# Router products with 32-column stationary matrices in the four quarters of the output partitions

## What is computed

```python
x = x + conv_ref(_ln_c(x), ...)       # sign of the centred x, 3x3 binary convolution, batch norm over all images, relu
t = _to_tokens(x)                     # 3136 tokens of 128 channels in each image
t = t + ffn_ref(_ln_t(t), ...)

def ffn_ref(x, ...):                  # x: 32 x 3136 x 128
    weights = (jnp.einsum('bsd,do->bso', x, wr) + br)[..., 0]    # the router: one number for each token
    _, idx = jax.lax.top_k(weights, k)                           # k = 1568
    sel_idx = idx[:, :kk]                                        # kk = 1567 tokens in each image
    h = jax.nn.gelu(jnp.einsum('bkd,dh->bkh', sel, w1) + b1)     # 128 -> 512
    y = jnp.einsum('bkh,hd->bkd', h, w2) + b2                    # 512 -> 128
    y = y * w_sel[..., None]                                     # times the router's number
    processed = jnp.zeros_like(x).at[batch_idx, sel_idx].set(y)
    return processed + x
```

## Time and profile before

| | |
|---|---|
| unprofiled executions | 2337.59, 2347.46, 2359.03 us |
| profiled execution, its own time | 2349.64 us |
| its span, first to last instruction | 2347.8 us |
| mean granted TensorE clock | 0.961 |
| TensorE busy | 2133.6 us (91%) |
| VectorE, ScalarE, GpSimd busy | 68%, 52%, 40% |

### The profile page before, as it was taken

One profiled execution on the slowest core, in us unless ns is written; L12 is line 12 of the kernel. 1 busy time (PEld: TensorE's weight loads), 2 busy tenths in 40 slices (PEclk: granted clock), 3 DMA queues, 4 the chain that ended last, 5 costly groups with the idle time before them and its releaser, 6 DMA issues. The chain is left out here.

```text
span 2347.8 us, 37567 instructions
## 1 busy us (share of the span) xinstructions
PE 2133.6 (91%) x9515; PEld 1079.1 (46%) x9515; DVE 1605.5 (68%) x4759; ACT 1219.9 (52%) x2030; POOL 944.6 (40%) x714
## 2 busy tenths in 40 slices
PE   6999999975999989899999989999999898989996
PEld 3555555542444444444444444444444444444442
DVE  6777777765667767667676766666666676767765
ACT  4444444434555555555555555565555555555553
POOL 1000000015455555555455545454555555545533
PEclk9999999997999999999999999999999999999998
DMA  4444444440232222223232223222223232223213
GB/s 148 165 164 159 155 156 156 154 164 26 95 117 101 101 101 101 107 107 106 105 115 101 101 101 126 96 108 101 102 101 115 107 116 101 101 101 112 101 61 114
DMA packets 68758, 268.17 MB, mean 114 GB/s; under 512 B 22352, under 2 KB 27184, under 8 KB 64688
## 3 DMA queue, kind: packets, MB, share of 16 engines
q1 hardware_dynamic: 59296, 215.50, 25.3%
q10 hardware_dynamic: 9360, 51.69, 6.0%
HBM read 188.08 MB, written 77.87 MB: 113 GB/s over the span
## 5 line engine op out<-in xcount | busy, mean ns | idle before, releaser
L943 PE MATMUL ps<-hs,w_c 128*128 128x448 f32 x1792 | 797.4, 571 | 0.6 <-ACT yo L505 0.6
L495 ACT ACTIVATE hs<-ps,b1c,undo 128x448 f32<-128x448 f32 x896 | 601.3, 719 | 166.6 <-PE ps L934 166.4
L412 POOL TENSOR_TENSOR tl<-tr,th 128x448 f16<-128x448 f32 x224 | 248.5, 1110 | 580.9 <-ACT th L525 472.3
L943 PEld LDWEIGHTS ps<-hs,w_c 128*128 128x128 f32 x1792 | 328.5, 198 | 218.0 <-issue 178.9
L860 PE MATMUL ps<-yo,cwT 128*128 128x448 bf16 x2016 | 425.7, 356 | 0.0
L505 ACT ACTIVATE yo<-ps,cols 128x448 f32<-128x448 f32 x224 | 141.8, 633 | 408.5 <-PE ps L943 408.3
L419 POOL TENSOR_TENSOR yo<-yo,base 128x448 f32<-128x448 f32 x224 | 285.9, 1282 | 134.0 <-DVE yo L787 134.0
L932 PE MATMUL ps<-th,w_h 128*128 128x448 f16 x896 | 326.0, 364 | 0.0
L934 PE MATMUL ps<-th,w_l 128*128 128x448 f16 x896 | 324.9, 363 | 0.0
L933 PE MATMUL ps<-tl,w_h 128*128 128x448 f16 x896 | 324.4, 362 | 0.0
L693 DVE TENSOR_TENSOR ur<-xb,ps 128x448 f32<-128x448 f32 x224 | 138.5, 619 | 263.9 <-PE ps L923 249.2
(11 more groups left out here) (125 smaller groups left out, 2578.0 us busy)
## 6 DMA issues: line engine op xcount, KB each, us to landing
xb<-x SPq DMA_DIRECT2D x31, 1568.0 KB, 7.5
xb<-x SPq DMA_DIRECT2D x33, 896.0 KB, 4.7
gate_all<-gate_row ACTq DMA_DIRECT2D x32, 896.0 KB, 4.4
result<-yo SPq DMA_DIRECT2D x32, 896.0 KB, 3.9
y_int<-y SPq DMA_DIRECT2D x32, 784.0 KB, 3.7
xb<-x SPq DMA_DIRECT2D x33, 672.0 KB, 4.4
gate_all<-gate_row ACTq DMA_DIRECT2D x32, 672.0 KB, 5.6
result<-yo SPq DMA_DIRECT2D x32, 672.0 KB, 3.0
```

The lines of the kernel that those rows point to most:

```text
L412: nc.gpsimd.tensor_tensor(cut(tl, c), tr[(b + c) % 2][:, :], cut(th, c), ALU.subtract).then_inc(tl_ready, 1)
L495: nc.scalar.activation(hs[(b + slot) % 2][:, j, :], ps[:, H_BANK + j, 0:T], ACT.Gelu_apprx_tanh, bias=b1c[:, j:j + 1], scale=undo[:, 1:2]) ...
L943: last = M(bank, w2_c[:, j, :], hs[(b + c) % 2][:, j, :], start=first, stop=final)
```

## The change

The stationary matrices of the router become 32 columns wide (COLS), cut from `wsel_h` and `wsel_l` of 64 columns. The seven chunks are taken in two parts: chunks 0 to 3 at position 17 and chunks 4 to 6 at position 25. Within a part, chunk q writes to the output partitions 32q to 32q + 31 of the same bank, and the four (or three) chunks are issued one behind the other for each of the three pairs of operands. Part 0 leaves its results on partitions 0, 32, 64, 96, part 1 on 1, 33, 65. `take_router` copies all 128 partitions, at position 26 instead of 28. The write of `wrow` to DRAM becomes two DMAs, of four and of three rows that lie 32 partitions apart, and the queue waits for both. The number of products stays 21.

```diff
+COLS = 32
+NQ = C // COLS
-ROUTER_AT = [15, 16, 17, 20, 21, 23, 27]
+ROUTER_AT = [17, 25]
-        wsel_h = sb("wsel_h", [C, 2 * C], f16)
+        wsel_h = sb("wsel_h", [C, 2 * COLS], f16)
-        wrow = sb("wrow", [NCH, T], f32)
+        wrow = sb("wrow", [C, T], f32)
...
-                    sp.dma_start(w_dram[bass.ds(n, 1), :].rearrange("a (c t) -> (a c) t", t=T),
-                                 wrow[:, :]).then_inc(w_saved, 16)
-                    sp.wait_ge(w_saved, (n + 1) * 16)
+                    for part in range(2):
+                        count = min(NQ, NCH - part * NQ)
+                        sp.dma_start(w_dram[bass.ds(n, 1), part * NQ * T:(part * NQ + count) * T]
+                                     .rearrange("a (c t) -> (a c) t", t=T),
+                                     wrow[part:part + (count - 1) * COLS + 1:COLS, :]).then_inc(w_saved, 16)
+                    sp.wait_ge(w_saved, (n + 1) * 32)
...
-                V.tensor_scalar(wrow[:, :], ps[0:NCH, T_BANK, 0:T], undo[0:NCH, 0:1], br_c[0:NCH, :],
+                V.tensor_scalar(wrow[:, :], ps[:, T_BANK, 0:T], undo[:, 0:1], br_c,
                                 ALU.mult, ALU.add).then_inc(w_taken, 1)
...
-            def router(n, b, c):
+            def router(n, b, part):
-                pe.wait_ge(tl_ready, n * NCH + c + 1)
-                if c == 0 and has(n - 1):
+                chunks = range(part * NQ, min(NCH, (part + 1) * NQ))
+                pe.wait_ge(tl_ready, n * NCH + chunks[-1] + 1)
+                if part == 0 and has(n - 1):
                     pe.wait_ge(mask_step, (n - 1) * MASK_STEPS + 3)
-                bank = ps[:, T_BANK, 0:T]
                 for i, (w, t) in enumerate(((wsel_h, th), (wsel_h, tl), (wsel_l, th))):
-                    last = M(bank, w[:, C - c:2 * C - c], cut(t, c), start=c == 0 and i == 0,
-                             stop=c == NCH - 1 and i == 2)
-                if c == NCH - 1:
+                    for q, c in enumerate(chunks):
+                        last = M(ps[q * COLS:(q + 1) * COLS, T_BANK, 0:T], w[:, COLS - part:2 * COLS - part], cut(t, c),
+                                 start=part == 0 and i == 0, stop=c + NQ >= NCH and i == 2)
+                if part == 1:
                     last.then_inc(w_done, 1)
```

More of the change, by code:

```diff
@@ L112, in block_kernel @@
         cb_c, gamma_c, beta_c, b2_c, wr_c, br_c = (cols[:, i:i + 1] for i in range(6))
-        wsel_h = sb("wsel_h", [C, 2 * C], f16)
-        wsel_l = sb("wsel_l", [C, 2 * C], f16)
+        wsel_h = sb("wsel_h", [C, 2 * COLS], f16)
+        wsel_l = sb("wsel_l", [C, 2 * COLS], f16)
         wr_s = sb("wr_s", [C, 1], f32)
@@ L617, in _ @@
             V.tensor_copy(w1_h[:, :], w1_s[:, :])
-            link(V.tensor_copy(wsel_h[:, C:C + 1], wr_s[:, :]))
+            link(V.tensor_copy(wsel_h[:, COLS:COLS + 1], wr_s[:, :]))
             V.tensor_tensor(w1_l[:, :], w1_s[:, :], w1_h[:, :], ALU.subtract)
-            link(V.tensor_tensor(wsel_l[:, C:C + 1], wr_s[:, :], wsel_h[:, C:C + 1], ALU.subtract))
+            link(V.tensor_tensor(wsel_l[:, COLS:COLS + 1], wr_s[:, :], wsel_h[:, COLS:COLS + 1], ALU.subtract))
             link(V.scalar_tensor_tensor(lo_c, br_c, -1.0, br_c, ALU.mult, ALU.max))
@@ L715, in take_router @@
                 if has(n - 1):
-                    dve.wait_ge(w_saved, n * 16)
-                V.tensor_scalar(wrow[:, :], ps[0:NCH, T_BANK, 0:T], undo[0:NCH, 0:1], br_c[0:NCH, :],
+                    dve.wait_ge(w_saved, n * 32)
+                V.tensor_scalar(wrow[:, :], ps[:, T_BANK, 0:T], undo[:, 0:1], br_c,
                                 ALU.mult, ALU.add).then_inc(w_taken, 1)
```

## The result

The changed kernel takes 2360.62 us in the median of 19 executions (2356.52 to 2367.34), the kernel before 2346.02 us in 19 (2331.92 to 2359.03). The ratio is 1.0062, with a 95% interval of 1.0045 to 1.0079: a little slower, about 15 us. The prediction was 2278 us and faster.

The account below looks back on a forecast made before the run. TensorE bounds the kernel, except from L908 to L952, where a chain outside it does. 31 turns of -2.53 + 0.40 = -2.13 us give -66 us, the last image about -3 us: 2278 us, range 2243 to 2325.

Parts of the forecast that it names:

- products, count to L908: From the search's first count to L908: 18 products (3.40 us) removed, part 0 (0.87 us) added, 2.53 us less per turn.
- signs named in advance: Signs of being wrong: starts 0.19 us apart, L908 waiting for L678, clock below 0.94 or over 0.98, second stretch 13.5 us or more.
- The quarters work at the same time: Router products at position 17: four column quarters overlap, so part 0's twelve products take three rounds, 0.87 us with switches.
- The rival that had it otherwise: Router products: quarters don't overlap, part 0 takes 3.67 us, 2368 us in all, 2428 with whole records; chance 12%.
- The Trainium skill's rule behind that rival: Router products: weight loads overlap with products in flight only where the row group differs; all four quarters share all rows.
- The second write, 0.40 us: `wrow` to DRAM, on the chain before the search: 0.32 us issue plus some 0.08 between issues, +0.40 us per turn.
- The bound of 0.8 us: Upper bound for the second write of `wrow`: the issue of one DMA of `rows` (4.90 / 6).
- Is L908 held by something else then?: At L908, which needs `rm` from L678: of 1.86 us slack 0.73 us stay, so the 2.53 us saving holds.
- The chain outside TensorE: From L908 to L952: pieces, six DMAs, `wrow` write, read and count bind; an added link costs its full length.
- The wait of part 1 for `tl`: Position 25: part 1 waits some 0.3 us for chunk 6's `tl`, covered by 1.88 us idle ahead of L921; cost nothing.
- The copy of 128 partitions: VectorE's `take_router`: the same 448 elements on each partition, 0.73 us as before, taken as nothing.
- The clock, taken as unchanged: TensorE's granted clock, 0.96 over 1600 us: idle 0.6 us shorter ahead of L921, 0.4 longer ahead of the search, no change.

Follow-up runs that it names:

- Experiment 1: The kernel before, with only the write of `wrow` split into two DMAs of neighbouring rows (partitions 0 to 3 and 4 to 6): 2388.78 us, ratio 1.0174.
- experiment 2: The kernel before, with VectorE's copy of all 128 partitions and the change's two writes of rows 32 partitions apart, router products as before: 2400.26 us, ratio 1.0228.
- after_clear: The changed kernel with two residual additions moved later and GpSimd's low part of chunk 5 held until the mean over deviation: median 2328.23 us of four, ratio 0.9862.
- residual_late: The changed kernel with the residual additions of chunks 2 and 3 moved from positions 18 and 22 to 25 and 27: 2333.67 us, ratio 0.9917.
- one_write: The changed kernel with the seven rows 16 partitions apart in one write and all 21 router products at position 25: 2353.33 us, ratio 1.0035.
- two_writes: The kernel before, with only the write of `wrow` as two DMAs of four and three neighbouring rows: 2388.78 us, ratio 1.0174.

## Why the prediction was wrong

Per turn, in us, from the table and from L914's waits:

| term | predicted | measured |
|---|---|---|
| products, count to L908 | -2.53 | -2.62 |
| second write | +0.40 | +1.25 |
| VectorE's rounding held by GpSimd | not seen | +0.94 |
| six DMAs of the rows' pieces | 0 | +0.13 |
| L914 waits for the mean over deviation | 0 | +0.54 |
| half clock and the rest | 0 | +0.44 |
| turn | -2.13 | +0.68 |

The measured turn is 56.49 - 55.81. L914's waits are (23.9 - 8.5) - (9.4 - 8.5) = 14.5 us over 27 turns, the 8.5 us being that of the start. The last term is what is left, so that the sum is exact by construction; up to 0.37 us of it are the half-clock time within the first stretch, which rose from 2.88 to 3.61 us in each turn. Two of the signs named in advance came: L908 waits for L678, and the second stretch is over 13.5 us.

- *The quarters work at the same time*: right, and the cost too, 0.78 us for part 0 against 0.87. The rival that had it otherwise gave 2368 us, close to the measured 2360.62, by a mechanism that the trace refutes: the sum of other losses happened to be as large, which is chance. The Trainium skill's rule behind that rival (TensorE: Matmul & The Clock Gate, Part 3: Packing small matmuls) does not hold here: the loads of the second four start 0.02 us after the first four products, with the same rows.
- *The second write, 0.40 us*: right as a mechanism and mis-sized by 0.85 us. The row that I read it from, the existing write, reads neighbouring partitions. Experiment 1 gives 0.34 us for such a write, experiment 2 gives 1.25 us for the change's. The bound of 0.8 us was too low as well: it was the issue of one added DMA, and I left the existing write at its old price, though it too now steps 32 partitions.
- *"Is L908 held by something else then?"*: this is the step that failed. It ends in "the saving holds, with 0.7 us to spare". The slack was computed from the order of the instructions and from their durations of before. It came to 0.73 us, and the trace after has 0.25 on average, with L914 waiting 1.9 us where all three operations are in the way. GpSimd and VectorE were treated as independent unless a semaphore joins them. GpSimd's power ends at 1242.40, and L678 was to start less than 0.5 us later, in the very stretch in which GpSimd works off what had queued behind its power. The rounding behind it, whose output the six DMAs wait for, was costed at its old 0.26 us, and measured 1.20 on average. That is the largest term that the sum does not have, and with L914's waits it is 1.48 us of the 2.81 us in each turn by which the prediction missed.
- *"The chain outside TensorE"* was read rightly as the bound of the second stretch, and that is why both errors, 0.85 us at the write and 0.94 us at the rounding, came through in full.
- *The wait of part 1 for `tl`*: 6.0 us in all, some 0.3 us where it occurs, under cover, as worked out. The copy of 128 partitions takes 0.726 us, as that of 7 did.
- *The clock, taken as unchanged*: 0.96 became 0.95 and half-clock time rose from 126 to 167 us. A longer chain did not only add its own length, but there is no fixed rate: in experiment 1 it was 11 us of chain and 37 us of time, in experiment 2 it was 39 and 53. What the clock costs shows from execution to execution of the kernel before, too: in 19 of them, 0.01 less of granted clock goes with some 21 us more (correlation -0.90). Part of what I had put down to the write in my theory of experiment 1 (+35 to +45 us at 1.27 us for each image) agreed with the time for the wrong reason: the link was 0.34 us.

## What to carry to other kernels

Where one engine's work is cut short, look at what the next small instructions on the critical chain share with engines that have no semaphore in common with them: a VectorE instruction of 0.2 us can be 3 us long if it lands in GpSimd's backlog, and the earlier it comes, the longer it is, until its own inputs hold it. Ask of such an instruction its shortest, median and longest duration over all images before its price is taken from one row. Before a result is spread over partitions for TensorE's sake, price how it is gathered again. Put work that must be done into stretches in which the engine waits for DMAs: all router products at position 25, GpSimd held back, one write and filled idle time together made 0.9637 out of 1.0062; how much of that each part is worth, the quarters included, no run separates.

## What the runs showed of the hardware that was not expected

- VectorE's `rm` instruction (112x28, two inputs in SBUF) waits through several consecutive GpSimd operations: 0.18 us with GpSimd idle (after_clear), 0.65 us behind the rest of one operation and 2.00 behind two (residual_late), 3.09 behind three (changed, one_write). The profile shows the wait as duration: VectorE's busy time rose by 59 us with the same instructions.
- A write from rows 32 partitions apart takes the queue 0.61 us for four rows and 0.76 us for three, one from seven rows 16 apart 0.79 us, against 0.31 and 0.24 us for four and three neighbouring rows and 0.32 us for seven (medians of the changed kernel, one_write, two_writes and before).
- Twelve divided products of 448 columns took 0.78 us, 65 ns each, against 189 ns undivided, with both switches in it.
- Useless products in idle time paid: 0.5 and 0.8% faster, with the clock between 700 and 2300 us at 0.99 instead of 0.96 and 0.95.
